# Latent attention of a four-layer kernel: queries four pairs ahead instead of eight, turn of the next rows in slot 2, second keys in slot 5

## The chip, the cores and the metric

The kernel runs on one core of one Trainium2 chip, with float32 data in and out. The metric is the device time in microseconds (us) of one execution. The engines are TensorE (PE in the rows; its weight loads are PEld), VectorE (DVE), ScalarE (ACT), GpSimd (POOL) and SyncE (SP, which issues the transfers). Each runs its own list of instructions in order and waits on semaphores.

## The reference

Four layers work on x of 4 x 256 tokens x 256 features. Each layer adds an attention-like step and a feed-forward step, each behind its own layer norm and gate. The parts around the change are the second layer's:

```python
def _L1_xattn_ref(hidden_q, kv_c, Wq, w_kc_q, w_kc_kv, W_qr, W_kr, Wo):
    ...
    q_r = jnp.einsum('bshq,hqr->bhsr', q_big, W_qr)
    k_r = jnp.einsum('bld,hdr->bhlr', kv_rope, W_kr)
    scores = jnp.einsum('bhsr,bhlr->bhsl', q_r, k_r)
    attn = jax.nn.softmax(scores, axis=-1)
    ctx_c = jnp.einsum('bhsl,bld->bhsd', attn, kv_rope)
    ctx_lat = jnp.einsum('bhsd,hkd->bshk', ctx_c, w_kc_kv)
    out = ctx_lat.reshape(b, s, H * K) @ Wo.T
    return out

def _L1_ffn_ref(x, w1, w2, w3):
    def _quantize(w):
        gamma = jnp.mean(jnp.abs(w))
        return jnp.clip(jnp.round(w / (gamma + EPS)), -1.0, 1.0)
    ...
    x1 = _bitlinear(x, w1)
    x2 = _bitlinear(x, w2)
    hidden = jax.nn.sigmoid(x1) * x2
    return _bitlinear(hidden, w3)
...
x = x + jnp.tanh(g_xattn[1]) * _L1_xattn_ref(_layernorm(x, axis=-1), ctx_512, ...)
x = x + jnp.tanh(g_ffn[1]) * _L1_ffn_ref(_layernorm(x, axis=-1), L1_ffn_w1, L1_ffn_w2, L1_ffn_w3)
```

## The kernel before

The program runs in phases: a beginning, "moe" (first layer), "latent" (the attention above), "ternary" (the feed-forward above), and "late" (the last two layers). All work of a phase is in fixed lists, one for each engine, written out in loops. The tables `latent_fills` and its like say which of the eight PSUM banks a step fills and in which order, and the semaphores `filled` and `drained` count the fills and their evacuations.

**The latent phase** has 4 batches x 8 pairs of heads = 32 items (`ITEMS1`), n = 8b + p. For item n, TensorE computes the queries of the pair (L1676, from the folded weights NW and the transposed rows XT), the scores (L1692, banks 0/1 or 2/3), the turned probabilities (L1708, eight transposes, banks 4 and 5), the values (L1720, bank 6) and the output (L1735, accumulated over the eight pairs in bank 7). VectorE takes the maximum (L1237), waits for ScalarE's four exponentials (L827), takes the reciprocal (L1244) and multiplies (L1246). ScalarE also evacuates the turned probabilities, the outputs of the values and the queries (all L710). The loop of TensorE for slot n is: turned(n), values(n-1), scores(n+2), sometimes a turn, query(n+8), output(n-2). VectorE works at n+2 in slot n: maximum(n+2), then exactly one scale(n+2).

**A turn** is the way in for the next batch: VectorE's statistics of a batch's rows (`stats`, L1013 to L1017), GpSimd's reciprocal root (`rstd`, L562 and L564), VectorE's normalised rows XN (L1025), four transposes (L1664) and ScalarE's copy to XT (L745). In the loop a turn uses bank 6, as queries do. VectorE runs the statistics two slots before the turn and XN one slot before it. Batch 1's statistics, XN and turn are done before the loop. The last turn, of slot 20, is for the ternary phase: its rows are batch 0's, with batch 0's latent output added.

**The way into the phase** on TensorE is: keys of batches 0 and 1 (four transposes, L1655), queries 0 and 1, scores 0, queries 2 and 3, scores 1, the turn of batch 1, the keys of batches 2 and 3, queries 4 to 7. Then comes the loop, whose turned(0) waits for VectorE's product 0 and for the evacuation of query 7.

**GpSimd** has one list too. In it, the `rstd` of the ternary phase's first rows comes right ahead of the ternary weights: two memsets (L595), then twelve operations that compare w1, w2 and w3 with their thresholds and subtract the results (L603, L605, L609), then three that split batch 0's transposed rows in bfloat16 parts (L617, L619, L621). The ternary phase's first matmul, `up1(0)` (L1752), stands in slot 31 of the latent loop, behind output(29) and ahead of values(31). It waits for all twelve operations and for the parts:

```python
            for b in range(NB):
                rstd(next_no("latent", b))
            pool.wait_ge(filled[6], fill("moe", 6, NB - 1, 0))
            for v in VC:
                pool.memset(v, 0.0).then_inc(pads_set, 1)
...
                if g == 0:
                    pe.wait_ge(ternary_ready, 12)
                if k == 0:
                    pe.wait_ge(parts_ready, b + 1)
```

Of the kernel before, what the change touches and what calls it, by code (L numbers as in the profile page):

```python
# [26 lines left out]
NB = 4  # L27
# [9 lines left out]
PAIRS0 = -(-CH0 // 2)  # L37
# [19 lines left out]
TURN_AT = 11  # L57
# [52 lines left out]

PAIRS1 = NH // 2
ITEMS1 = NB * PAIRS1
Q_AHEAD = PAIRS1
TURN1_AT = 4


def latent_fills():


    order = [(7, "kr", 0, 0), (4, "q", 0, 0), (5, "q", 0, 1), (0, "s", 0, 0), (4, "q", 0, 2), (5, "q", 0, 3),  # L120
             (2, "s", 0, 1), (7, "turn", 0, 0), (6, "kr", 1, 0)]
    order += [(4 + i % 2, "q", 0, i) for i in range(4, PAIRS1)]
    for n in range(ITEMS1 + 2):
        if n < ITEMS1:
            order.append((4, "t", n // PAIRS1, n % PAIRS1))
        if 1 <= n <= ITEMS1:
            order.append((6, "o", (n - 1) // PAIRS1, (n - 1) % PAIRS1))
        if n + 2 < ITEMS1:
            order.append((2 * (n % 2), "s", (n + 2) // PAIRS1, (n + 2) % PAIRS1))
        if n % PAIRS1 == TURN1_AT and n // PAIRS1 + 1 < NB:  # L130
            order.append((6, "turn", n // PAIRS1 + 1, 0))
        if n + Q_AHEAD < ITEMS1:
            order.append((6, "q", (n + Q_AHEAD) // PAIRS1, n % PAIRS1))
        if n >= 2 and (n - 2) % PAIRS1 == 0:
            order.append((7, "y", (n - 2) // PAIRS1, 0))
    return order
# [140 lines left out]
def build(nc, a, out):  # L277
    with ExitStack() as ctx:
# [404 lines left out]
        def _(act):  # L683
# [157 lines left out]
                evacuate("latent", "o", n // PAIRS1, n % PAIRS1, (OT1[:, n % 2, :], PS[:, 6, 0:S]))  # L841

            keys_out(0)
            for m in range(4):
                query_out(m)
            exponents(0)
            latent_turned(0)
            keys_out(1)
            for m in (4, 5):
                query_out(m)  # L850
            exponents(1)
            for m in range(6, PAIRS1):
                query_out(m)
            for n in range(ITEMS1 + 1):
                if n < ITEMS1:
                    turned_out(n)
                if n:
                    outputs_out(n - 1)
                if n % PAIRS1 == TURN1_AT and n // PAIRS1 + 1 < NB:
                    latent_turned(n // PAIRS1 + 1)  # L860
                if n + Q_AHEAD < ITEMS1:
                    query_out(n + Q_AHEAD)
                if n + 2 < ITEMS1:
                    exponents(n + 2)
                if n == ITEMS1 - 1:
                    hidden_tanh(0)
# [119 lines left out]
        def _(dve):  # L986
# [150 lines left out]
            for b in range(NB):  # L1137
                bank, value = fill_at("moe", "router", b)
                dve.wait_ge(filled[bank], value)
                dve.tensor_reduce(NMAX[:, :], PS[:, 7, 0:2 * E0].rearrange("p (a e) -> p a e", a=2), AX, ALU.max,  # L1140
                                  negate=True).then_inc(nmax_ready, 1)
                dve.wait_ge(drained[bank], value)
                link(dve.reciprocal(RZ[:, :], Z[:, :]))
                for i in range(2):
                    last = dve.tensor_scalar(SC[:, i, 0:E0], EX[:, i, :], RZ[:, i:i + 1], None, ALU.mult)
                link(last)
                for i in range(2):
                    last = dve.max(T8[:, i, :], SC[:, i, 0:E0])
                link(last)

                link(dve.memset(T8[:, :, K0:8], LOW))
                for i in range(2):
                    last = dve.match_replace(REP[:, i, :], T8[:, i, :], SC[:, i, :], 0.0)
                link(last)
                link(dve.tensor_tensor(CM[:, :, 0:E0], SC[:, :, 0:E0], REP[:, :, 0:E0], ALU.subtract))
                link(dve.tensor_reduce(SU[:, :], CM[:, :, 0:E0], AX, ALU.add))
                link(dve.tensor_scalar(SU[:, :], SU[:, :], 1e-20, None, ALU.add))
                link(dve.reciprocal(SU[:, :], SU[:, :]))
                for i in range(2):
                    last = dve.tensor_scalar(CM[:, i, 0:E0], CM[:, i, 0:E0], SU[:, i:i + 1], 0.5,  # L1160
                                             ALU.mult, ALU.mult)
                link(last)

                link(dve.tensor_copy(C3[:, :, 0:PART], CM[:, :, :]))
                link(dve.tensor_tensor(REP[:, :, 0:PART], CM[:, :, :], C3[:, :, 0:PART], ALU.subtract))
                link(dve.tensor_copy(C3[:, :, PART:2 * PART], REP[:, :, 0:PART]))
                dve.tensor_tensor(C3[:, :, 2 * PART:3 * PART], REP[:, :, 0:PART], C3[:, :, PART:2 * PART],
                                  ALU.subtract).then_inc(comb_ready, 1)
                for c in range(PAIRS0):
                    g, m, n = c % 2, P, 512  # L1170
                    if c == PAIRS0 - 1:
                        m, n = F0 % P, S
                    dve.wait_ge(tanh_ready, b * PAIRS0 + c + 1)
                    dve.scalar_tensor_tensor(gated[0:m, 0:n], tanh_g[0:m, g, 0:n], 1.0, PS[0:m, g, 0:n],
                                             ALU.add, ALU.mult).then_inc(drained[g], 1)
                    dve.wait_ge(drained[g], fill("moe", g, b, c // 2))
                    dve.wait_ge(filled[2 + g], fill("moe", 2 + g, b, c // 2))
                    dve.tensor_tensor(hidden[0:m, 0:n], gated[0:m, 0:n], PS[0:m, 2 + g, 0:n], ALU.mult) \
                        .then_inc(drained[2 + g], 1)
                    dve.wait_ge(drained[2 + g], fill("moe", 2 + g, b, c // 2))  # L1180
                    dve.wait_ge(filled[4 + g], fill("moe", 4 + g, b, c // 2))

                    if c >= 2:
                        dve.wait_ge(h_used, b * (PAIRS0 - 1) + c - 1)
                    dve.tensor_tensor(H[0:m, g, :, :].rearrange("p a s -> p (a s)")[:, 0:n], hidden[0:m, 0:n],  # L1185
                                      PS[0:m, 4 + g, 0:n], ALU.mult).then_inc(drained[4 + g], 1)
                    if b + 1 < NB:

                        if c == 0:
                            stats(b + 1)  # L1190
                        for r in ROUNDS_AT.get(c, ()):
                            graph_round(b + 1, r)
                        if c == 4:
                            graph_norm(b + 1)
                        if c == 7:
                            graph_mask(b + 1)
                        if c == GRAPH_AT - 1:
                            graph_add(b + 1)
                    else:
                        if c == 2:  # L1200
                            weight_sums()
                        if c == GRAPH_AT - 1:
                            thresholds()
                    if c == GRAPH_AT - 1:
                        stats((b + 1) % NB)
                    if c == GRAPH_AT:
                        normalise(after_moe(b), (b + 1) % NB,
                                  fill_at("moe", "turn", b - 1)[1])
                    if b == NB - 1 and c == TURN_AT:
                        stats(1)  # L1210
                    if b == NB - 1 and c == PAIRS0 - 1:
                        latent_next(0)
                add_residual("moe", b, TG[:, 4:5])
            v_total[0] = done[0] + done[1]

# [38 lines left out]
            for n in range(ITEMS1 + 2):  # L1254
                b, p = n // PAIRS1, n % PAIRS1
                if n + 2 < ITEMS1:
                    latent_maximum(n + 2)
                    if p == TURN1_AT - 2 and b + 1 < NB:
                        stats((b + 2) % NB)
                    if p == TURN1_AT - 1 and b + 1 < NB:  # L1260
                        latent_next(b + 1)
                    latent_scale(n + 2)
                if PAIRS1 <= n < ITEMS1 and p == 1:
                    output("latent", b - 1, TG[:, 1:2])
# [199 lines left out]
        def _(pe):  # L1464
# [232 lines left out]
            def latent_turned(n):  # L1697
# [1 line left out]
                pe.wait_ge(probs_scaled, n + 1)  # L1699
                bank = begin("latent", "t", n // PAIRS1, n % PAIRS1)  # L1700
                if n == 0:
                    at_, query = fill_at("latent", "q", 0, PAIRS1 - 1)
                    pe.wait_ge(drained[at_], query)
                for e in range(2):
                    for t in range(2):
# [72 lines left out]
            latent_query(2)  # L1778
            latent_query(3)
            latent_scores(1)  # L1780
            latent_turn(0)
            latent_keys(1)
            for m in range(4, PAIRS1):
                latent_query(m)
            for n in range(ITEMS1 + 2):
                if n < ITEMS1:
                    latent_turned(n)
# [1 line left out]
                    latent_values(n - 1)  # L1789
                if n + 2 < ITEMS1:  # L1790
                    latent_scores(n + 2)
                if n % PAIRS1 == TURN1_AT and n // PAIRS1 + 1 < NB:
                    latent_turn(n // PAIRS1 + 1)
                if n + Q_AHEAD < ITEMS1:
                    latent_query(n + Q_AHEAD)
                if n >= 2:
# [346 lines left out]
```

## Time and profile before

| what | us |
|---|---|
| median of 3 runs (lowest, highest) | 828.22 (827.05, 830.11) |
| the profiled execution, its own time | 828.94 |
| its span, first to last instruction | 826.9 |
| TensorE busy | 785.8 (95%) |
| VectorE, ScalarE, GpSimd busy | 504.7, 357.5, 155.0 |
| mean granted clock of TensorE | 0.983 of full |

The profile is of one execution. Its rows give the start in us from the span's start, the duration, the engine, the line, the operation, and in brackets how long the engine was idle before it and for whom. A row can merge several instructions (x8), and its duration then runs over all of them. TensorE's matmuls are pipelined, so the start of the next row is the better end of a row. The latent phase lies between 342 and 518 us.

### The profile page before, as it was taken

Reading aid. Unit: us, or ns where it says so; the run is one execution under the profiler, and the core shown is the slowest. Engines: PE = TensorE matmul, PEld = TensorE weight load, DVE = VectorE, ACT = ScalarE, POOL = GpSimd, SP = SyncE. Lnnn points to the kernel's source line nnn. Section 1 sums busy time; section 2 is a strip of 40 time slices with the busy share of each in tenths; the row PEclk is TensorE's granted clock in tenths of the full one; section 3 lists DMA queues with packets and bytes.
Section 4 is the critical chain, followed back from the end, with each engine's and each line's share of the span. In section 5 each row is a group of like instructions: output and inputs, shape, how many; then the busy total and the mean of one; then the engine's idle time right before and its main releaser. Section 6 shows DMA issues by size and latency. Waiting matters only on the chain.

```text
span 826.9 us, 13605 instructions
## 1 busy us (share of the span) xinstructions
PE 785.8 (95%) x5086; PEld 607.9 (74%) x5086; DVE 504.7 (61%) x1187; ACT 357.5 (43%) x1175; POOL 155.0 (19%) x160
## 2 busy tenths in 40 slices
PE   6899999999999999989999789999999999999984
PEld 3678888888888888866767556787667776777663
DVE  5656555965886564555656764333777856756763
ACT  2121112101111101366767466222888867767751
POOL 0000021000000000000002990223244332332110
PEclk9989999999999999999999899999999999999998
DMA  8945100000002000320000000000000000000000
GB/s 248 337 152 200 34 0 1 1 1 1 0 1 105 1 1 0 130 66 1 1 1 2 1 1 1 1 2 1 2 1 2 1 2 2 2 1 2 14 15 25
DMA packets 16177, 28.06 MB, mean 34 GB/s; under 512 B 3648, under 2 KB 11824, under 8 KB 15856
## 3 DMA queue, kind: packets, MB, share of 16 engines
q1 hardware_dynamic: 16112, 27.19, 10.1%
q8 instruction: 41, 0.67, 0.4%
q14 instruction: 24, 0.20, 0.1%
HBM read 26.13 MB, written 1.05 MB: 33 GB/s over the span
## 4 chain that ended last, share of the span: by engine, by line
PE 84%; DVE 7%; ACT 6%; issue 2%; POOL 1%; DMA 0%; POOLq 0%; SPq 0%; ACTq 0%; DVEq 0%
PE PS L1584 21%; PE PS L1608 10%; PE PS L1820 6%; PE PS L1844 5%; PE PS L1752 4%; PE PS L1676 3%; PE PS L1870 3%; ACT arena L827 3%; PE PS L1767 3%; PE PS L1692 2%; PE PS L1720 2%; PE PS L1708 2%; PE PS L1735 2%; PE PS L1933 2%; DVE arena L1246 2%
## 5 line engine op out<-in xcount | busy, mean ns | idle before, releaser
L710 ACT ACTIVATE arena<-PS 128x256 f32<-128x256 f32 (+3 forms) x192 | 103.2, 561 | 77.6 <-PE PS L1676 37.4
L562 POOL TENSOR_TENSOR RS<-MV,eps 128x2 f32<-128x2 f32 x32 | 6.3, 196 | 578.5 <-DVE MV L1017 517.5
L897 ACT ACTIVATE arena<-PS,W_d 128x256 f32<-128x256 f32 (+1 forms) x256 | 111.2, 453 | 6.6 <-DVE W_d L1291 6.0
L770 ACT ACTIVATE tanh_g<-PS 128x512 f32<-128x512 f32 x48 | 28.7, 599 | 180.8 <-PE PS L1584 180.8
L1584 PE MATMUL PS<-XT,W_g 128*128 128x256 f32 (+1 forms) x400 | 97.4, 386 | 0.0
L1584 PE MATMUL PS<-XT,W_u 128*128 128x256 f32 (+1 forms) x400 | 95.4, 381 | 0.0
L1608 PE MATMUL PS<-W_d,mlp_tmp 128*128 128x256 f32 (+1 forms) x400 | 94.1, 379 | 0.0
L1185 DVE TENSOR_TENSOR mlp_tmp<-mlp_tmp,PS 128x512 f32<-128x512 f32 (+1 forms) x52 | 34.7, 667 | 82.7 <-PE PS L1595 82.2
L1584 PEld LDWEIGHTS PS<-XT,W_u 128*128 128x128 f32 (+1 forms) x400 | 76.1, 190 | 11.0
L1584 PEld LDWEIGHTS PS<-XT,W_g 128*128 128x128 f32 (+1 forms) x400 | 75.2, 192 | 10.7 <-issue 0.8
L1608 PEld LDWEIGHTS PS<-W_d,mlp_tmp 128*128 128x128 f32 (+1 forms) x400 | 72.2, 190 | 8.7
L827 ACT ACTIVATE arena<-PS,arena 128x256 f32<-128x256 f32 x128 | 59.0, 478 | 13.2 <-DVE arena L1237 11.2
L1844 PE MATMUL PS<-ident,arena 128*128 128x128 f32 x448 | 61.2, 277 | 0.0
L1844 PEld LDWEIGHTS PS<-ident,arena 128*128 128x128 f32 x448 | 48.9, 141 | 10.6 <-issue 10.2
L897 ACT ACTIVATION_READ_ACCUMULATOR arena<-PS,W_d 128x1 f32 x256 | 54.3, 212 | 0.0
L1301 DVE COPY arena<-PS 128x512 f32<-128x512 f32 (+1 forms) x64 | 39.5, 617 | 14.8 <-PE PS L1844 14.8
L1291 DVE TENSOR_REDUCE W_d<-PS 128x4 f32<-128x1024 f32 x32 | 39.1, 1221 | 13.9 <-PE PS L1820 13.8
L1246 DVE TENSOR_TENSOR arena<-arena 128x1024 f32<-128x1024 f32 x32 | 44.4, 1389 | 1.1
L1237 DVE TENSOR_REDUCE arena<-PS 128x4 f32<-128x1024 f32 x32 | 39.1, 1222 | 9.0 <-PE PS L1692 6.8
L1244 DVE RECIPROCAL arena<-arena 128x4 f32<-128x4 f32 x32 | 5.7, 177 | 59.9 <-ACT arena L827 59.9
L1676 PE MATMUL PS<-XT,NW 128*128 128x256 f32 x128 | 35.6, 408 | 4.0 <-ACT XT L745 2.5
L1708 PE MATMUL PS<-ident,arena 128*128 128x128 f32 x256 | 34.4, 278 | 4.0 <-DVE arena L1246 2.8
(213 smaller groups left out, 1377.1 us busy)
## 6 DMA issues: line engine op xcount, KB each, us to landing
W_d<-in_w_d SPq DMA_DIRECT2D x1, 3072.0 KB, 10.5
arena<-in_wq SPq DMA_DIRECT2D x4, 512.0 KB, 7.2
arena<-in_wo1T SPq DMA_DIRECT2D x4, 512.0 KB, 9.0
W_g<-in_w_g SPq DMA_DIRECT2D x2, 1024.0 KB, 12.3
W_u<-in_w_u SPq DMA_DIRECT2D x2, 1024.0 KB, 14.2
arena<-in_wkq1T SPq DMA_DIRECT2D x4, 384.0 KB, 8.2
mlp_w<-in_w SPq DMA_DIRECT2D x1, 1408.0 KB, 6.0
W_g<-in_w_g SPq DMA_DIRECT2D x1, 1120.0 KB, 8.7
```

Source lines behind the costliest of these rows:

```text
L710: last = act.activation(dst, src, ACT.Copy)
L827: last = act.activation(PR[:, n % 2, k * S:(k + 1) * S], PS[:, bank + e, i * S:(i + 1) * S], ACT.Exp, bias=NM1[:, n % 2, k:k + 1], accum_o ...
L897: last = act.activation(PL[:, n % 2, k * S:k * S + w], PS[:, bank + x, i * S:i * S + w], ACT.Exp, bias=NML[:, n % 2, k:k + 1], accum_out=D ...
L1237: dve.tensor_reduce(NM1[:, n % 2, :], PS[:, bank:bank + 2, :].rearrange("p e (i s) -> p (e i) s", i=2), AX, ALU.max, negate=True).then_inc ...
L1246: dve.tensor_tensor(rows, rows, DEN1[:, n % 2, :].unsqueeze(2).to_broadcast([P, 4, S]), ALU.mult) \
L1301: dve.tensor_copy(PLT[:, n % 4, 512:512 + w], PS[:, bank, 0:w]).then_inc(drained[bank], 1)
L1584: last = mm(PS[0:m, k, e * S:(e + 1) * S], w[:, d, f0:f0 + m], XT[p][:, d, :], start=d == 0, stop=d == 1)
L1608: last = mm(PS[:, 6, i * D:(i + 1) * D], H[0:m, c % 2, e, i * P:(i + 1) * P], W_d[0:m, f, :], start=f == 0 and i == 0, stop=f == CH0 - 1, ...
L1676: last = mm(PS[:, bank, 0:S], NW[:, c, i * P:(i + 1) * P], XT[b % 2][:, c, :], start=c == 0, stop=c == 1)
L1708: last = pe.transpose(PS[:, bank + e, t * S + i * P:t * S + (i + 1) * P], PR[:, n % 2, col:col + P], ident[:, :])
L1820: last = mm(PS[:, bank + x, i * S:i * S + w], QM[r % 2][rows, e, c, i * P:(i + 1) * P], keys[rows, c, 0:w], start=i == 0 or not causal(r), ...
L1844: last = pe.transpose(PS[:, bank + x, t * S + (i - first) * P:t * S + (i - first + 1) * P], PL[:, n % 2, col:col + P], ident[:, :])
```

## The change

`Q_AHEAD` goes from 8 to 4: query(n+4) stands in slot n's place of query(n+8), and queries 4 to 7 move from the way in to slots 0 to 3. `TURN1_AT` goes from 4 to 2, and a turn stands in each of the four batches: slots 2, 10, 18 and 26. The turns are for batch 1, batch 2, batch 3 and the ternary phase's first rows. Before, the last three of them were in slots 4, 12 and 20. The keys of batches 2 and 3 move from the way in to slot 5 (bank 6). VectorE's statistics and XN move with the turns: slots 0, 8, 16, 24 and 1, 9, 17, 25. Batch 1's leave the end of the moe phase. GpSimd's list keeps its order; what it waits for moves.

```diff
-Q_AHEAD = PAIRS1
-TURN1_AT = 4
+Q_AHEAD = 4
+TURN1_AT = 2
+KEYS1_AT = 5
...
-             (2, "s", 0, 1), (7, "turn", 0, 0), (6, "kr", 1, 0)]
-    order += [(4 + i % 2, "q", 0, i) for i in range(4, PAIRS1)]
+             (2, "s", 0, 1)]
...
 (ScalarE)
-            for m in range(4):
+            for m in range(3):
                 query_out(m)
             exponents(0)
-            latent_turned(0)
-            keys_out(1)
-            for m in (4, 5):
-                query_out(m)
+            query_out(3)
             exponents(1)
-            for m in range(6, PAIRS1):
-                query_out(m)
...
 (VectorE, end of moe)
-                    if b == NB - 1 and c == TURN_AT:
-                        stats(1)
-                    if b == NB - 1 and c == PAIRS0 - 1:
-                        latent_next(0)
...
 (VectorE, latent loop)
-                    if p == TURN1_AT - 2 and b + 1 < NB:
-                        stats((b + 2) % NB)
-                    if p == TURN1_AT - 1 and b + 1 < NB:
-                        latent_next(b + 1)
+                    if p == TURN1_AT - 2:
+                        stats((b + 1) % NB)
+                    if p == TURN1_AT - 1:
+                        latent_next(b)
...
 (TensorE)
             latent_scores(1)
-            latent_turn(0)
-            latent_keys(1)
-            for m in range(4, PAIRS1):
-                latent_query(m)
...
-                if n % PAIRS1 == TURN1_AT and n // PAIRS1 + 1 < NB:
-                    latent_turn(n // PAIRS1 + 1)
+                if n % PAIRS1 == TURN1_AT and n < ITEMS1:
+                    latent_turn(n // PAIRS1)
+                if n == KEYS1_AT:
+                    latent_keys(1)
                 if n + Q_AHEAD < ITEMS1:
                     latent_query(n + Q_AHEAD)
```

In the listings below the changed kernel's lines are 5 lower on TensorE and VectorE's loop (L1703 is L1708 of before, L1671 is L1676, L1659 is L1664, L1232 is L1237, L1239 is L1244, L1241 is L1246, L1224 is L1229) and 1 lower for the statistics and XN (L1024 is L1025).

TensorE on the way into the phase, before, from scores 1 to slot 1's turned probabilities:

```order
L1692 MATMUL PS<-KR,arena 128x256 x4
L1664 MATMUL PS<-ident,XN 128x128 x4
L1655 MATMUL PS<-ident,VV 128x128 x4
L1676 MATMUL PS<-XT,NW 128x256 x8
L1708 MATMUL PS<-ident,arena 128x128 x8
L1692 MATMUL PS<-KR,arena 128x256 x4
L1676 MATMUL PS<-XT,NW 128x256 x2
L1708 MATMUL PS<-ident,arena 128x128 x8
```

The same place in the changed kernel, up to the first turn:

```order
L1687 MATMUL PS<-KR,arena 128x256 x4
L1703 MATMUL PS<-ident,arena 128x128 x8
L1687 MATMUL PS<-KR,arena 128x256 x4
L1671 MATMUL PS<-XT,NW 128x256 x2
L1703 MATMUL PS<-ident,arena 128x128 x8
L1715 MATMUL PS<-arena,VV 64x256 x4
L1687 MATMUL PS<-KR,arena 128x256 x4
L1671 MATMUL PS<-XT,NW 128x256 x2
L1703 MATMUL PS<-ident,arena 128x128 x8
L1715 MATMUL PS<-arena,VV 64x256 x4
L1687 MATMUL PS<-KR,arena 128x256 x4
L1659 MATMUL PS<-ident,XN 128x128 x4
```

Between scores 1 and turned(0), the turn, the keys and eight matmuls of four queries are gone; the first turn comes behind scores 4 in slot 2.

VectorE in slots 24 and 25 (maximum 26 to maximum 28), before:

```order
L1237 TENSOR_REDUCE arena<-PS 128x4
L1244 RECIPROCAL arena<-arena 128x4
L1246 TENSOR_TENSOR arena<-arena 128x1024
L1237 TENSOR_REDUCE arena<-PS 128x4
L1244 RECIPROCAL arena<-arena 128x4
L1246 TENSOR_TENSOR arena<-arena 128x1024
L1229 SCALAR_TENSOR_TENSOR X<-PS,TG,X 128x512
L1237 TENSOR_REDUCE arena<-PS 128x4
```

The same place in the changed kernel, from maximum 26 to product 27:

```order
L1232 TENSOR_REDUCE arena<-PS 128x4
L1012 BN_STATS BN<-X 128x6
L1013 BN_STATS BN<-X 128x6
L995 MEMSET carrier 128x1
L1015 BN_AGGR MV<-BN 128x2
L1016 BN_AGGR MV<-BN 128x2
L1239 RECIPROCAL arena<-arena 128x4
L1241 TENSOR_TENSOR arena<-arena 128x1024
L1232 TENSOR_REDUCE arena<-PS 128x4
L1024 TENSOR_SCALAR XN<-X,MV,RS 128x256 x2
L1239 RECIPROCAL arena<-arena 128x4
L1241 TENSOR_TENSOR arena<-arena 128x1024
```

The statistics of the ternary phase's first rows, which before stood behind maximum 20 (slot 18), stand behind maximum 26 (slot 24), and their XN behind maximum 27.

## Rows read from the trace of the kernel before

**Rows 1.** The page: its first line, and the chain of waits by engine.

```profile
span 826.9 us, 13605 instructions
PE 84%; DVE 7%; ACT 6%; issue 2%; POOL 1%; DMA 0%; POOLq 0%; SPq 0%; ACTq 0%; DVEq 0%
```

**Rows 2.** Timeline, TensorE, way into the phase: start, us, engine, line, operation, count, [idle].

```profile
348.72 0.66 PE L1664 MATMUL PS<-ident,XN 128*128 128x128 f32 x4
...
349.64 3.62 PE L1676 MATMUL PS<-XT,NW 128*128 128x256 f32 x16
...
354.48 1.06 PE L1708 MATMUL PS<-ident,arena 128*128 128x128 f32 x8 [1.21 <-ACT arena L710]
```

**Rows 3.** Timeline, VectorE, way into the phase: product 0.

```profile
350.22 1.22 DVE L1246 TENSOR_TENSOR arena<-arena 128x1024 f32<-128x1024 f32 x1
```

**Rows 4.** Timeline, TensorE, slots 4 (with a turn) and 5 of the loop.

```profile
375.54 0.66 PE L1664 MATMUL PS<-ident,XN 128*128 128x128 f32 x4
376.88 1.13 PE L1676 MATMUL PS<-XT,NW 128*128 128x256 f32 x4 [0.69 <-ACT XT L745]
377.85 1.03 PE L1735 MATMUL PS<-PM,arena 128*128 128x256 f32 x4
378.71 1.04 PE L1708 MATMUL PS<-ident,arena 128*128 128x128 f32 x8
...
383.58 1.04 PE L1708 MATMUL PS<-ident,arena 128*128 128x128 f32 x8
```

**Rows 5.** Timeline, TensorE, slots 25 and 26, which have no query.

```profile
485.86 1.09 PE L1708 MATMUL PS<-ident,arena 128*128 128x128 f32 x8 [0.35 <-DVE arena L1246]
...
490.44 1.09 PE L1708 MATMUL PS<-ident,arena 128*128 128x128 f32 x8 [0.35 <-DVE arena L1246]
```

**Rows 6.** Timeline, VectorE, from the ternary phase's statistics (slot 18) on.

```profile
449.55 0.15 DVE L1017 BATCH_NORM_AGGREGATE MV<-BN 128x2 f32<-128x6 f32 x1
...
453.11 7.24 DVE L1025 TENSOR_SCALAR XN<-X,MV,RS 128x256 f32<-128x256 f32 x2
...
460.47 4.06 DVE L1246 TENSOR_TENSOR arena<-arena 128x1024 f32<-128x1024 f32 x1
...
477.60 3.62 DVE L1246 TENSOR_TENSOR arena<-arena 128x1024 f32<-128x1024 f32 x1
```

**Rows 7.** Timeline, GpSimd, first, second and fifth operation of the ternary weights, last of the parts.

```profile
450.69 1.85 POOL L595 MEMSET W_d<- 128x1024 f32 x2
452.51 3.85 POOL L603 TENSOR_SCALAR mlp_tmp<-mlp_w,thr 128x1408 f32<-128x1408 f32 x1
...
463.55 4.69 POOL L603 TENSOR_SCALAR mlp_tmp<-mlp_w,thr 128x1408 f32<-128x1408 f32 x1
...
493.98 2.01 POOL L621 TENSOR_TENSOR W_d<-mlp_tmp,W_d 128x512 bf16<-128x512 f32 x1
```

**Rows 8.** Timeline, TensorE, slots 19, 20 and 26: its longer waits, and up1(0).

```profile
448.55 1.04 PE L1708 MATMUL PS<-ident,arena 128*128 128x128 f32 x8
...
460.41 1.12 PE L1664 MATMUL PS<-ident,XN 128*128 128x128 f32 x4 [3.63 <-DVE XN L1025]
462.70 2.08 PE L1676 MATMUL PS<-XT,NW 128*128 128x256 f32 x4 [1.18 <-ACT XT L745]
464.57 1.65 PE L1735 MATMUL PS<-PM,arena 128*128 128x256 f32 x4
...
495.79 1.31 PE L1735 MATMUL PS<-PM,arena 128*128 128x256 f32 x4 [2.17 <-DVE X L1229]
...
518.39 1.47 PE L1752 MATMUL PS<-W_d 128*128 128x256 bf16 x12
```

**Rows 9.** Stretches: us, busy of PE, PEld, DVE, ACT, POOL, granted clock, DMA share, GB/s.

```profile
453.00:466.00 13.00, 8.19 (x40) 5.87 (x39) 12.63 (x6) 5.18 (x15) 12.82 (x4) 0.74 0.01 3
...
493.00:500.00 7.00, 4.83 (x24) 3.33 (x22) 4.36 (x6) 4.65 (x14) 2.84 (x3) 0.76 0.00 0
...
516.00:540.00 24.00, 24.00 (x172) 19.02 (x171) 8.61 (x26) 6.28 (x14) 4.73 (x7) 1.00 0.01 1
```

More of the change, by code:

```diff
@@ L129, in latent_fills @@
             order.append((2 * (n % 2), "s", (n + 2) // PAIRS1, (n + 2) % PAIRS1))
-        if n % PAIRS1 == TURN1_AT and n // PAIRS1 + 1 < NB:
-            order.append((6, "turn", n // PAIRS1 + 1, 0))
+        if n % PAIRS1 == TURN1_AT and n < ITEMS1:
+            order.append((6, "turn", n // PAIRS1, 0))
+        if n == KEYS1_AT:
+            order.append((6, "kr", 1, 0))
         if n + Q_AHEAD < ITEMS1:
-            order.append((6, "q", (n + Q_AHEAD) // PAIRS1, n % PAIRS1))
+            order.append((6, "q", (n + Q_AHEAD) // PAIRS1, (n + Q_AHEAD) % PAIRS1))
         if n >= 2 and (n - 2) % PAIRS1 == 0:
@@ L858, in _ @@
                     outputs_out(n - 1)
-                if n % PAIRS1 == TURN1_AT and n // PAIRS1 + 1 < NB:
-                    latent_turned(n // PAIRS1 + 1)
+                if n % PAIRS1 == TURN1_AT and n < ITEMS1:
+                    latent_turned(n // PAIRS1)
+                if n == KEYS1_AT:
+                    keys_out(1)
                 if n + Q_AHEAD < ITEMS1:
@@ L1701, in latent_turned @@
                 if n == 0:
-                    at_, query = fill_at("latent", "q", 0, PAIRS1 - 1)
+                    at_, query = fill_at("latent", "q", 0, Q_AHEAD - 1)
                     pe.wait_ge(drained[at_], query)
@@ L1791, in _ @@
                     latent_scores(n + 2)
-                if n % PAIRS1 == TURN1_AT and n // PAIRS1 + 1 < NB:
-                    latent_turn(n // PAIRS1 + 1)
+                if n % PAIRS1 == TURN1_AT and n < ITEMS1:
+                    latent_turn(n // PAIRS1)
+                if n == KEYS1_AT:
+                    latent_keys(1)
                 if n + Q_AHEAD < ITEMS1:
```

## The prediction, made before the run

> **What bounds the kernel now.** I read the page first: one chain of work ended last, and 84% of it is TensorE [rows 1]. So a stretch in which TensorE is never idle ends sooner only if it has less work, and any wait of TensorE that is added ahead of such a stretch is paid in full. Then I read the timeline of the latent phase engine by engine. Three things are to be seen there. On the way in, TensorE is busy from 348.72 to about 353.3, waits 1.21 us, and starts turned(0) at 354.48 [rows 2], although VectorE's product 0 ended at 350.22 + 1.22 = 351.44 [rows 3]. In the loop a slot with a query takes 383.58 - 378.71 = 4.87 us with TensorE never idle [rows 4], and one without a query 490.44 - 485.86 = 4.58 us, in which TensorE waits for VectorE [rows 5]. So the softmax chain (maximum, exponentials, product) has a period of 4.58, and a query costs 377.85 - 376.88 = 0.97 of TensorE. Last, GpSimd gets its long list of ternary weights when VectorE's statistics of slot 18 end, at 449.55 + 0.15 = 449.70 [rows 6], and ends it, with batch 0's parts, at 493.98 + 2.01 = 495.99 [rows 7]: 46.3 us. Its consumer, up1(0), starts at 518.39 [rows 8]. That is 22.4 us of slack, and it is what the change spends.
>
> **The way in.** Between scores 1 and turned(0) the turn, the keys and four queries are gone. Turned(0) can then start when product 0 is there, about 0.1 us behind 351.44, at 351.55: product 0 doesn't get earlier, since it stands behind maximum 1, which needs scores 1, and scores 1 keeps its place. Gain: 354.48 - 351.55 = 2.9 us. VectorE's statistics and XN that leave the end of the first phase are worth nothing, because TensorE is busy there; in slots 0 and 1 the exponentials hide them.
>
> In exchange TensorE is idle from 348.72 to 351.55, 2.8 us. The trace has idle times of 2.17 and 3.63 us in this phase [rows 8]; around both, the granted clock was 0.76 and 0.74 of full, that is partly at 1.2 GHz instead of 2.4 [rows 9]. The second one cost, beyond the wait, (1.12 - 0.66) + (2.08 - 1.13) + (1.65 - 1.03) = 2.0 us [rows 4, 8]. I expect the same fall here, between 0 and 2.0 us, and take 1.2, because the first slots have waits for ScalarE that can swallow some of it.
>
> **The turns and the keys.** In the loop a turn costs what stands between its start and that of the query behind it, 376.88 - 375.54 = 1.34 us, since the query needs bank 6 back from ScalarE [rows 4]. The first turn now is in the loop: +1.34. The keys are the same four transposes, copy and bank: +1.34. The other three turns only move (slots 4, 12, 20 to 10, 18, 26).
>
> **The queries.** Four of them leave the way in (in the 2.9 us above) and stand in slots 24 to 27 at the end. Each of these slots then takes 4.87 in place of 4.58: 4 x 0.29 = +1.2 us, if TensorE were the one that decides there. Without GpSimd the change would be close to nothing: -2.9 + 1.2 + 2.7 + 1.2 = +2.2 us.
>
> **GpSimd's list.** The statistics that release it move from slot 18 to slot 24. Where is slot 24's end in the changed kernel? Before, turned(19) started at 448.55 [rows 8], and the statistics ended 1.15 us after that. Turned(25) now starts at 448.55 - 2.9 (way in) + 6 x 4.87 (six slots more) + 1.34 (two turns lay ahead before, now three) + 1.34 (keys) + 1.2 (clock) = 478.7, and the statistics end at 479.9.
>
> How long does the list take? Before, 46.3 us, in which VectorE made seven products. A product and an operation of GpSimd don't run together: XN took 7.24 us, one product 4.06 and one 3.62, where they arrived just behind the start of an operation of GpSimd [rows 6], and GpSimd's comparison took 4.69 where it had a product ahead of it and 3.85 where it had not [rows 7]. So each product costs GpSimd 0.84 us. The list alone is 46.3 - 7 x 0.84 = 40.4; with the five products that now follow the statistics and its XN (27 to 31) it is 44.6, and I take 45.0. The end is 479.9 + 45.0 = 524.9, 6.5 us behind up1(0)'s 518.39.
>
> The Trainium skill says the same of the two engines ("SBUF — State Buffer", "Who interferes with whom"): whoever issues first holds the shared port pair for its whole instruction, and the other fully blocks. The trace agrees: XN's two instructions, 0.73 us elsewhere, took 7.24. By that rule GpSimd can't be stretched beyond the waits counted above, nor shortened below its own work.
>
> Is TensorE late there anyway? From 478.7 it needs 4.87 for slot 25; 4.87 + 1.34 + 6.1 for slot 26, which now has the turn that waits for XN as slot 20 did (3.63 idle, 1.18 - 0.69 more for XT, 2.0 of clock) [rows 4, 8]; 4.87 for slot 27; 3 x 4.58 for 28 to 30; and some 3.0 up to up1(0): 517.5. Then it waits 7.4 us. The products that meet an operation of GpSimd (about 2.4 us each: 3.62 - 1.22) use up this wait first. Idle time before up1(0) brings the lower clock again; I take the 2.0 us of above once more, bounds 0 and 2.8. From there on TensorE was busy for 24.00 of 24.00 us [rows 9], so nothing takes the delay back.
>
> **Sum.** +6.5 (up1(0) later) + 2.0 (clock behind the wait) = +8.5 us. Way in, turns and clock at the start are inside the 6.5. Against the profiled execution's own 828.94 this is 837.4; that execution was 0.7 above the median of 828.22, so 836.7.
>
> **Rivals.**
>
> 1. *GpSimd's list is at its shortest.* If the products cost it nothing because they fall into its gaps, it takes 40.4, and up1(0) is at 520.4. With no fall of the clock on the way in, 519.2. That is +0.8 to +2.0, plus clock 1 to 2: 830 to 832. For it: the products adapt to GpSimd's period. Against: 4.69 in place of 3.85 where a product came between. Chance 0.16.
>
> 2. *Faster: TensorE sets the end.* Then the gain on the way in counts and the fuller slots 24 to 27 cost little: 517.5 - 518.4 = -0.9, and without the fall of the clock on the way in -2.1: 826 to 827. The wait of 2.17 us for batch 2's output in slot 26 [rows 8], which is merged with the turn's wait, is in that sum. The point from which it decides: the list must take less than 517.5 - 479.9 = 37.6 us, which is below its own 40.4, or the statistics must end 3 us earlier than I think. Chance 0.05.
>
> 3. *Slower still: VectorE's chain ends behind GpSimd.* Each product that just misses its turn costs 2.4 to 3.5 us. With three or four such misses in slots 26 to 31, turned(31) is late and up1(0) is at 527 to 529, +10 to +12 with the clock: 838.5 to 841. Before there was one such product beside XN and the one behind it. Chance 0.12.
>
> 4. *The change doesn't do what it says*, for instance since the statistics still come early. The order shows them in slot 24; chance 0.01.
>
> **Numbers.** The forecast has 0.66: up1(0) waits for GpSimd's list, 833 to 840 with its bounds (clock 0 to 2.0 on the way in and 0 to 2.8 behind the wait, list 43 to 46.3). The range, 831 to 841, takes in most of rivals 1 and 3 and leaves out rival 2. About 0.5% (4.1 us) is what a measurement of this kernel can tell from no change: slower by more than that is above 832.4, which is the forecast and rival 3 and little of rival 1, 0.80; within is most of rival 1 and part of the others, 0.15; faster 0.05.
>
> **What would show it.** In the profile of the changed kernel: turned(0) at about 351.5, with about 2.8 us idle before it and a granted clock below 1 behind it; slots of 4.87 up to slot 27; statistics ending at about 480; XN of slot 25 at some 7 us; GpSimd's last part ending at about 525; TensorE idle for several us ahead of up1(0), and waiting for GpSimd; the ternary phase as long as before. The prediction is wrong if up1(0) starts without a wait for GpSimd, if the list takes under 40 us, or if the delay at up1(0) isn't found again in the span.

## The result, and the profile after

| | before | changed |
|---|---|---|
| median of 8 runs each | 829.22 (827.05 to 831.93) | 834.69 (829.55 to 835.28) |
| ratio, 95% interval | | 1.006 (1.0037 to 1.0083) |
| the profiled execution | 828.94, span 826.9 | 835.25, span 833.2 |

The change makes the kernel slower, by some 5 us; the interval lies above 1. The forecast was 836.7 in a range from 831 to 841. These are the rows of the changed kernel that answer to the ones ahead. First TensorE's timeline on the way in, at the keys of slot 5, at turned(25), in slots 26 to 29, and at up1(0) (columns as in [rows 2]; lines are 5 lower than before's):

```profile
342.17 0.60 PE L1650 MATMUL PS<-ident,VV 128*128 128x128 f32 x4
...
351.22 1.09 PE L1703 MATMUL PS<-ident,arena 128*128 128x128 f32 x8 [2.67 <-DVE arena L1241]
352.25 1.65 PE L1687 MATMUL PS<-KR,arena 64*128 64x256 f32 x8
353.82 2.07 PE L1671 MATMUL PS<-XT,NW 128*128 128x256 f32 x4
355.69 1.27 PE L1703 MATMUL PS<-ident,arena 128*128 128x128 f32 x8
...
380.02 0.66 PE L1650 MATMUL PS<-ident,VV 128*128 128x128 f32 x4
381.37 1.13 PE L1671 MATMUL PS<-XT,NW 128*128 128x256 f32 x4 [0.69 <-ACT KR L712]
...
478.53 1.04 PE L1703 MATMUL PS<-ident,arena 128*128 128x128 f32 x8
...
489.81 1.12 PE L1659 MATMUL PS<-ident,XN 128*128 128x128 f32 x4 [3.29 <-DVE XN L1024]
492.10 2.07 PE L1671 MATMUL PS<-XT,NW 128*128 128x256 f32 x4 [1.17 <-ACT XT L747]
494.75 2.04 PE L1730 MATMUL PS<-PM,arena 128*128 128x256 f32 x4 [0.57 <-DVE X L1224]
496.58 1.92 PE L1703 MATMUL PS<-ident,arena 128*128 128x128 f32 x8
498.43 1.60 PE L1715 MATMUL PS<-arena,VV 128*64 128x256 f32 x8
...
502.85 1.04 PE L1703 MATMUL PS<-ident,arena 128*128 128x128 f32 x8
...
509.23 1.52 PE L1703 MATMUL PS<-ident,arena 128*128 128x128 f32 x8 [2.21 <-DVE arena L1241]
510.68 1.98 PE L1715 MATMUL PS<-arena,VV 128*64 128x256 f32 x8
...
523.53 1.47 PE L1747 MATMUL PS<-W_d 128*128 128x256 bf16 x12 [1.61 <-issue]
```

Turned(0) starts at 351.22, 2.67 us after the last work of TensorE, and the score and query matmuls behind it are slow. The keys of slot 5 cost 381.37 - 380.02 = 1.35 us. Turned(25) starts at 478.53. The last row is up1(0), 5.1 us later than before's 518.39 [rows 8].

GpSimd's timeline, from the start of the list to the end of the parts (answers to [rows 7]), and VectorE's, from the statistics on (answers to [rows 6]):

```profile
480.11 1.84 POOL L597 MEMSET W_d<- 128x1024 f32 x2
481.93 3.84 POOL L605 TENSOR_SCALAR mlp_tmp<-mlp_w,thr 128x1408 f32<-128x1408 f32 x1
...
492.95 4.69 POOL L605 TENSOR_SCALAR mlp_tmp<-mlp_w,thr 128x1408 f32<-128x1408 f32 x1
...
522.28 1.15 POOL L623 TENSOR_TENSOR W_d<-mlp_tmp,W_d 128x512 bf16<-128x512 f32 x1
```

```profile
478.97 0.15 DVE L1016 BATCH_NORM_AGGREGATE MV<-BN 128x2 f32<-128x6 f32 x1
...
482.83 6.93 DVE L1024 TENSOR_SCALAR XN<-X,MV,RS 128x256 f32<-128x256 f32 x2
...
489.87 4.06 DVE L1241 TENSOR_TENSOR arena<-arena 128x1024 f32<-128x1024 f32 x1
...
498.06 3.82 DVE L1241 TENSOR_TENSOR arena<-arena 128x1024 f32<-128x1024 f32 x1
...
505.23 3.94 DVE L1241 TENSOR_TENSOR arena<-arena 128x1024 f32<-128x1024 f32 x1
```

The statistics end at 478.97 + 0.15 = 479.12, the list at 522.28 + 1.15 = 523.43, and up1(0) starts 0.1 us behind it: TensorE waits for GpSimd. XN took 6.93 us (7.24 before, in slot 19), and three products met an operation of GpSimd, where before it was two (4.06 and 3.62, [rows 6]).

Granted clock (columns as in [rows 9]) of the way in and of slot 26 with what follows:

```profile
348.00:360.00 12.00, 8.99 (x53) 6.02 (x50) 7.96 (x14) 7.49 (x25) 0.88 (x2) 0.86 0.63 212
...
488.00:500.00 12.00, 8.44 (x30) 5.61 (x30) 9.90 (x7) 4.42 (x12) 11.82 (x4) 0.57 0.00 0
```

The span grew by 6.3 us, and up1(0) came only 5.1 later. The rest comes later, nearly all of it at the very end of the program. From the chain of waits (start, us, what), the same eight matmuls of the last output projection, before and then changed:

```profile
804.55 2.01 PE PS L1933 x8
```

```profile
809.58 3.30 PE PS L1926 x8
```

Both have a wait of 0.83 us ahead. The granted clock of the 4 us there, before and then changed:

```profile
804.50:808.50 4.00, 3.22 (x16) 2.58 (x17) 2.90 (x12) 0.64 (x2) 0.00 (x0) 1.00 0.02 4
```

```profile
809.50:813.50 4.00, 3.92 (x12) 2.86 (x12) 1.73 (x8) 0.00 (x0) 0.00 (x0) 0.58 0.00 0
```

In one execution TensorE was at 2.4 GHz there, in the other mostly at 1.2. That is 1.29 us. The instructions there are the same in both kernels, and the time from up1(0) to the end was 308.0 to 310.1 us over all ten profiles of this text without following the length of the phase (310.1 in the first experiment below, 309.7 in the changed kernel). So I don't count these 1.29 us to the change; that is an argument from the profiles, no run tests it.

### The profile page after: what moved, and what is told of

Its sections match the earlier page's. It is cut to its first block, busy times and chain, and to the rows that moved or that the text cites. A ratio compares the mean times of both kernels' runs of the same rounds, so it can differ in the third digit from the quotient of the medians.

```text
span 833.2 us, 13605 instructions
## 1 busy us (share of the span) xinstructions
PE 790.2 (95%) x5086; PEld 611.2 (73%) x5086; DVE 508.0 (61%) x1187; ACT 356.1 (43%) x1175; POOL 152.9 (18%) x160
## 4 chain that ended last, share of the span: by engine, by line
PE 87%; DVE 6%; ACT 4%; issue 2%; POOL 1%; DMA 0%; POOLq 0%; SPq 0%; ACTq 0%; DVEq 0%
PE PS L1579 21%; PE PS L1603 10%; PE PS L1813 6%; PE PS L1837 5%; PE PS L1747 4%; PE PS L1671 4%; PE PS L1687 4%; PE PS L1715 3%; PE PS L1863 3%; PE PS L1703 3%; PE PS L1730 3%; PE PS L1762 3%; PE PS L1926 2%; PE PS L1590 1%; PE PS L1532 1%
## 5 line engine op out<-in xcount | busy, mean ns | idle before, releaser
L1241 DVE TENSOR_TENSOR arena<-arena 128x1024 f32<-128x1024 f32 x32 | 47.3, 1480 | 1.1
L1232 DVE TENSOR_REDUCE arena<-PS 128x4 f32<-128x1024 f32 x32 | 39.2, 1224 | 8.5 <-PE PS L1687 7.7
L1239 DVE RECIPROCAL arena<-arena 128x4 f32<-128x4 f32 x32 | 5.7, 177 | 59.2 <-ACT arena L829 59.2
L1671 PE MATMUL PS<-XT,NW 128*128 128x256 f32 x128 | 37.5, 420 | 4.3 <-ACT XT L747 3.2
L1703 PE MATMUL PS<-ident,arena 128*128 128x128 f32 x256 | 34.9, 281 | 5.6 <-DVE arena L1241 5.6
```

The lines of the kernel that those rows point to most:

```text
L1232: dve.tensor_reduce(NM1[:, n % 2, :], PS[:, bank:bank + 2, :].rearrange("p e (i s) -> p (e i) s", i=2), AX, ALU.max, negate=True).then_inc ...
L1241: dve.tensor_tensor(rows, rows, DEN1[:, n % 2, :].unsqueeze(2).to_broadcast([P, 4, S]), ALU.mult) \
L1671: last = mm(PS[:, bank, 0:S], NW[:, c, i * P:(i + 1) * P], XT[b % 2][:, c, :], start=c == 0, stop=c == 1)
L1703: last = pe.transpose(PS[:, bank + e, t * S + i * P:t * S + (i + 1) * P], PR[:, n % 2, col:col + P], ident[:, :])
```

## The experiments

The time up to the phase's first matmul varied by some 3.8 us between profiles (339.35 to 343.16), and the time from up1(0) to the end by 2.1 (308.0 to 310.1). So beside the times I read from each trace the **phase**: from the first keys (first row above; L1655 before) to up1(0). All from one profile of each kernel; the ratios are against the kernel before on the same chips. The phase too has parts that vary between executions: the clock on the way in is worth 1.4 us of it (see the part on the prediction), so small differences between phases are no more than hints.

| kernel | phase, us | median (runs) | ratio, 95% interval |
|---|---|---|---|
| before | 518.39 - 342.40 = 176.0 | | |
| changed | 523.53 - 342.17 = 181.4 | 834.69 (8) | 1.006 (1.0037 to 1.0083) |
| e1_last_turn_20 | 514.90 - 339.40 = 175.5 | 828.48 (12) | 1.0004 (0.999 to 1.0018) |
| e2_queries_only | 512.92 - 339.35 = 173.6 | 827.75 (12) | 0.9982 (0.9965 to 1.0) |
| e3_list_behind_xn | 525.31 - 341.43 = 183.9 | 838.89 (4) | 1.0123 (1.0085 to 1.0161) |
| e4_short_list | 520.09 - 343.16 = 176.9 | 829.14 (10) | 1.0013 (0.9998 to 1.0027) |
| e5_before_list_behind_xn | 514.96 - 341.83 = 173.1 | 825.06 (6) | 0.9957 (0.9941 to 0.9973) |
| e6_q4_wait | 512.83 - 342.10 = 170.7 | 823.42 (6) | 0.9934 (0.9915 to 0.9953) |
| e6_q5_wait | 514.17 - 343.10 = 171.1 | 824.31 (6) | 0.9947 (0.9931 to 0.9962) |
| e6_q6_wait | 513.33 - 341.54 = 171.8 | 825.84 (8) | 0.997 (0.9954 to 0.9985) |

### The last turn alone put back

```diff
+TURNS1 = {2: 0, 10: 1, 18: 2, 20: 3}
...
-                if n % PAIRS1 == TURN1_AT and n < ITEMS1:
-                    latent_turn(n // PAIRS1)
+                if n in TURNS1:
+                    latent_turn(TURNS1[n])
```

The same edit stands in ScalarE's loop and the table of fills; VectorE's `stats` and `latent_next` go by `n + 2 in TURNS1` and `n + 1 in TURNS1`.

> The changed kernel with one thing put back: the last turn (the ternary phase's first rows) is in slot 20 again, with its statistics in slot 18 and its XN in slot 19; the other turns stay in slots 2, 10 and 18, the second keys in slot 5, queries four ahead. Theory (GpSimd's list, released by those statistics, sets up1(0)): the list is released near 449 us and ends near 496, so up1(0) no longer waits for it; up1(0) starts near 520.5 instead of 523.5, the time is 2 to 3 us below the changed kernel's, ratio to before about 1.003. Rival (the turns, keys and queries that stand in the loop cost the time by themselves, and the list only happens to end late): up1(0) stays at 523 or later and the ratio stays at 1.006.

Measured: phase 175.5, ratio 1.0004. GpSimd's list and TensorE's up1(0), from their timelines:

```profile
445.85 1.84 POOL L598 MEMSET W_d<- 128x1024 f32 x2
...
490.25 1.16 POOL L624 TENSOR_TENSOR W_d<-mlp_tmp,W_d 128x512 bf16<-128x512 f32 x1
```

```profile
514.90 1.47 PE L1748 MATMUL PS<-W_d 128*128 128x256 bf16 x12
```

The list ends 23.5 us ahead of up1(0), which doesn't wait. The last turn, moved by six slots, makes a difference of 181.4 - 175.5 = 5.9 us. Of these, 1.4 are the clock on the way in, which stayed high in this execution, long before the turn that was moved; the 4.5 that are left agree with the ratios (1.006 against 1.0004, some 4.6 us), and that is nearly all of the loss. The 2 to 3 us that I had expected were too few: I had counted the low clock on the way in as lost here too, and also full slots 24 to 27, but these took 499.44 - 478.76 = 20.7 us from turned(24) to turned(28), against 502.36 - 481.28 = 21.1 before. The wait of 2.17 us for batch 2's output [rows 8] is down to 0.60 in this kernel.

### The queries alone

```diff
-Q_AHEAD = PAIRS1
+Q_AHEAD = 4
...
-            for m in range(4, PAIRS1):
+            for m in range(4, Q_AHEAD):
                 latent_query(m)
```

With the same bounds in the table of fills and in ScalarE's list; the turn and the keys stay on the way in.

> The kernel before with the queries alone changed: four pairs ahead instead of eight. The turn of batch 1 and the second keys stay on the way in, the other turns in slots 4, 12 and 20. Theory: turned(0) starts 2.9 us earlier, near 351.5, behind 1.9 us of idle time; slots 24 to 27 hold a query again (+1.2 us at most); GpSimd's list starts 2 to 3 us earlier and is never waited for; up1(0) starts at 516.7 to 518.5, ratio 0.998 to 1.001. Rival (queries four ahead are what costs, since they fill slots 24 to 27 or lower the clock on the way in): up1(0) at 521 or later, ratio 1.003 or more.

Measured: phase 173.6, ratio 0.9982. TensorE, end of the way in:

```profile
346.16 0.60 PE L1655 MATMUL PS<-ident,VV 128*128 128x128 f32 x4
348.44 1.09 PE L1708 MATMUL PS<-ident,arena 128*128 128x128 f32 x8 [1.69 <-DVE arena L1246]
```

Turned(0) comes 348.44 - 339.35 = 9.1 us after the first keys; before it was 354.48 - 342.40 = 12.1. Of this gain of 3.0 us, 2.4 are left at up1(0), so in the loop the queries cost 0.6 us net. It is made of two parts. Slots 24 and 25 took 486.53 - 475.53 = 11.0 us, against 490.44 - 481.28 = 9.2 before; that is 1.8 us, more than I had put for all four queries. Most of it comes back behind slot 25, where the wait for batch 2's output is 0.61 us instead of 2.17 [rows 8] and the clock doesn't fall behind it:

```profile
491.31 1.10 PE L1735 MATMUL PS<-PM,arena 128*128 128x256 f32 x4 [0.61 <-DVE X L1229]
492.25 1.04 PE L1708 MATMUL PS<-ident,arena 128*128 128x128 f32 x8
```

The interval reaches 1.0, so by the time alone this is not told from no change. The profiled execution was the shortest of the twelve (823.41 us); its phase began 3.0 us earlier than before's, which the phase's own length doesn't hold. The first experiment has one turn and the keys more in the loop than the second, and its turns of batches 2 and 3 stand six slots later. From turned(0) to turned(19), that is before GpSimd's list, it takes 445.07 - 348.46 = 96.6 us against 443.03 - 348.44 = 94.6, and the phases differ by 175.5 - 173.6 = 1.9. So the turn and the keys cost 1.9 to 2.0 us in the loop, against the 2.7 in the sum.

### GpSimd's list later still

```diff
             pool.wait_ge(filled[6], fill("moe", 6, NB - 1, 0))
+            pool.wait_ge(xn_ready, next_no("latent", NB - 1) + 1)
             for v in VC:
                 pool.memset(v, 0.0).then_inc(pads_set, 1)
```

> The changed kernel, in which GpSimd starts its list of ternary weights only when VectorE has written the XN of slot 25. XN and GpSimd's comparison then don't meet: XN takes 0.7 us instead of 6.9, and TensorE's waits in slot 26 (3.3 for XN, part of 1.2 for XT) and the low clock behind them go. Theory (the list sets up1(0)): TensorE gains some 5 us and nothing comes of it; the list starts and ends 3.5 us later, near 527, up1(0) starts there and waits 8 us or more, and the time is 3 to 5.5 us above the changed kernel's (ratio to before 1.010 to 1.013). Rival (TensorE's waits for VectorE in slots 26 to 31 set the end): the time falls by 4 to 5 us, ratio 1.000 to 1.001.

Measured: phase 183.9, ratio 1.0123. VectorE's XN, GpSimd's list and TensorE's up1(0):

```profile
482.23 0.73 DVE L1025 TENSOR_SCALAR XN<-X,MV,RS 128x256 f32<-128x256 f32 x2
```

```profile
483.07 1.84 POOL L598 MEMSET W_d<- 128x1024 f32 x2 [3.52 <-DVE XN L1025]
...
524.06 1.15 POOL L624 TENSOR_TENSOR W_d<-mlp_tmp,W_d 128x512 bf16<-128x512 f32 x1
```

```profile
525.31 2.72 PE L1748 MATMUL PS<-W_d 128*128 128x256 bf16 x12 [9.08 <-issue]
527.96 1.44 PE L1716 MATMUL PS<-arena,VV 128*64 128x256 f32 x8
```

XN is at its own 0.73 us, TensorE no longer waits for it, and the kernel is slower: TensorE's time went into a wait of 9.08 us. That is the test that tells the theories apart, and the rival, 1.000, is out. The medians are 4.2 us apart, as expected; the phases only 2.5, from one profile each. The clock behind the wait was low: up1(0) and the values took 2.65 and 1.37 us from start to start, where they take 1.40 and 1.01 in the changed kernel, 1.6 us together.

### A shorter list

```diff
+                some = 64 if k == 1 else n
-                pool.tensor_scalar(less[0:parts, 0:n], wf, thr[0:parts, 1, c:c + 1], None, ALU.is_lt) \
+                pool.tensor_scalar(less[0:parts, 0:some], wf[:, 0:some], thr[0:parts, 1, c:c + 1], None, ALU.is_lt) \
```

The second comparison likewise.

> The changed kernel with a shorter list on GpSimd: the two comparisons of the second half of w1 and w2 work on 64 of their 1408 columns, so the weights of the ternary phase are not the reference's. It is for the price of the list. Theory: the list gets 7 us shorter, ends near 516, and TensorE's own chain decides; up1(0) starts at 518 to 522, and the time is 1.5 to 5 us below the changed kernel's (ratio 1.000 to 1.004). Rival (the list isn't waited for): no change against the changed kernel, ratio 1.006.

Measured: phase 176.9, 4.4 us below the changed kernel's; ratio 1.0013. GpSimd's last operation is over at 518.05, 2.0 us before up1(0) at 520.09, which now has no wait:

```profile
516.03 2.02 POOL L624 TENSOR_TENSOR W_d<-mlp_tmp,W_d 128x512 bf16<-128x512 f32 x1
```

```profile
520.09 1.47 PE L1748 MATMUL PS<-W_d 128*128 128x256 bf16 x12
```

So TensorE's own chain is nearly the kernel before's length (176.0), and what is above it in the changed kernel is the list, by its wait of 1.61 us and by the products that the full list delays. Behind XN's own, the products that met an operation of GpSimd took 2.43 us here (the one at 505.44), and 3.82 and 3.94 in the changed kernel.

### The same wait where the list has slack

The edit of the third experiment, in the kernel before.

> The kernel before with one wait added: GpSimd starts its list of ternary weights only when VectorE has written the XN of slot 19. It is the wait of the run e3_list_behind_xn, put where the list has slack. Theory (the list matters only once its slack is spent; here it has 22 us): the list starts and ends 3.5 us later, near 499, and still isn't waited for; XN takes 0.7 instead of 7.2 us, TensorE's 3.6 us for it and the low clock behind go; the phase from the first keys to up1(0), 176.0 before, takes 170 to 172, ratio 0.993 to 0.996. Rival (TensorE's wait for XN is made up elsewhere in the phase): 175 to 176, ratio 1.000.

Measured: phase 173.1, ratio 0.9957, faster. VectorE's XN and products (timeline), with those that pass freely left out:

```profile
452.47 0.73 DVE L1026 TENSOR_SCALAR XN<-X,MV,RS 128x256 f32<-128x256 f32 x2
...
461.51 2.48 DVE L1247 TENSOR_TENSOR arena<-arena 128x1024 f32<-128x1024 f32 x1
467.33 4.04 DVE L1247 TENSOR_TENSOR arena<-arena 128x1024 f32<-128x1024 f32 x1
...
479.33 3.90 DVE L1247 TENSOR_TENSOR arena<-arena 128x1024 f32<-128x1024 f32 x1
```

One wait on GpSimd makes the kernel slower where the list is due (1.0123 against 1.006) and faster where it isn't. Slot 20 took 459.72 - 453.01 = 6.7 us from turned(20) to turned(21), against 466.06 - 453.67 = 12.4 before. The phase gained only 2.9 us, half of that: three products now meet an operation of GpSimd for long (2.48, 4.04, 3.90), where before it was two (4.06, 3.62). The phase is 1 us above the theory's range and 2 below the rival's; I had taken the later list for harmless to the products.

### Both gains together, and how many queries ahead

```diff
-Q_AHEAD = PAIRS1
+Q_AHEAD = 4
...
+            pool.wait_ge(xn_ready, next_no("latent", NB - 1) + 1)
```

With the other bounds as in the second experiment; the other two kernels have 5 and 6.

> Queries four ahead alone (as in e2_queries_only, phase 173.6) together with GpSimd's wait for XN. Theory: the two gains add, since one is on the way in and the other at slot 20: phase 167.5 to 169.5, ratio 0.990 to 0.993. Rival: the products that meet the later list lose the gain again, 171 or more, ratio 0.995 or more.

> As e6_q4_wait with queries five ahead: query 4 stays on the way in, in 0.9 of the 1.7 us in which TensorE waits for product 0. Theory: turned(0) starts as early, and one query less stands in the loop (0.97 us of TensorE where it decides): phase 0 to 0.7 us below e6_q4_wait's. Rival: nothing, since slot 27's query fits under the softmax chain anyway.

> As e6_q4_wait with queries six ahead: queries 4 and 5 on the way in. TensorE's wait for product 0 is then filled (1.8 us), but turned(0) also waits for ScalarE's copy of query 5, which stands behind four exponentials, the XT copy and the keys. Theory: turned(0) starts up to 0.5 us later than with four, the phase is within 0.7 us of e6_q4_wait's. Rival: the exponentials of pair 1, behind two copies more, come 0.8 us later and delay slots 1 and 2: phase 0.5 to 1 us longer.

Measured: phases 170.7, 171.1 and 171.8; ratios 0.9934, 0.9947, 0.997. The phase gains add, 176.0 - 2.4 - 2.9 = 170.7, though the phase fell less than I had expected, as in the fifth experiment. By the ratios the sum is not told from the wait alone (0.9915 to 0.9953 and 0.9941 to 0.9973 overlap). More queries on the way in don't help. Six cost 1.1 us of the phase against four, more than the 0.7 I had allowed and near the rival's 0.5 to 1. With six, turned(0) comes 9.71 us after the first keys instead of 9.09 and waits for ScalarE's copy. With five it comes at 9.09, and the phase isn't shorter, so the query left over was not what decided. The intervals of four and five overlap; four with the wait has the lowest median here, and its interval is below both the kernel before's 1 and the changed one's.

## Why the prediction was right, and where its sum was off

**GpSimd's list sets up1(0): right.** Its release at 479.12 (forecast 479.9), its length 523.43 - 479.12 = 44.3 us (forecast 45.0), up1(0) at 523.53 (forecast 524.9). The way there held too: turned(0) at 351.22, of which 0.2 us is an earlier start of the phase, the keys at 1.35 us, turned(25) at 478.53 (forecast 478.7). The first and third experiment show the cause: with the last turn alone put back the loss is gone, and a later list costs more although TensorE loses its waits for XN.

**The clock on the way in: right in this profile.** In the changed kernel's profile the score matmuls took 1.65 us (1.13 in the first experiment) and the query 2.07 (1.13 in [rows 4]); from turned(0) to turned(1) it was 355.69 - 351.22 = 4.5 us, against 351.51 - 348.46 = 3.1 us in the first experiment, where after the same wait the clock did not fall (last section). At turned(18) it is still 1.4 us (443.05 - 351.22 = 91.8 against 438.85 - 348.46 = 90.4), so nothing swallowed it. The price is 1.4 us (forecast 1.2), and it comes and goes: that it was paid in the profiled execution was luck for the forecast of 479.9.

**Slots 24 to 27, and the loop: too dear.** The queries were put at 1.2 us and cost 0.6 net, turn and keys at 2.7 and cost 1.9 to 2.0 (first and second experiment). The term for the queries had no part for the wait of 2.17 us for batch 2's output and the low clock behind it, of which 0.61 us and no low clock were left in the second experiment. The first slots have room of their own, since TensorE waits for ScalarE there (0.53 us at 355.16 in the first experiment, 0.92 at 355.53 in the second); that this is why the turn and the keys cost less isn't shown by a run.

**TensorE ready at 517.5: wrong, and with it the term of 2.0 us for the clock.** TensorE was ready at 523.53 - 1.61 = 521.9, 4.4 us later than forecast. By the forecast's own steps turned(26) was due at 483.6 and came at 483.40. Turned(28) was due at 500.8 and came at 502.85, and it had no wait ahead: the first 2.1 us are mostly the low clock in slots 26 and 27. I had put 2.0 us for it, as in slot 20, where it was over with the output; here output, turned and values took 1.83, 1.85 and 1.52 us from start to start too, so that it cost 3.8. The rest are two products that met the list (3.82 and 3.94 us, 2.6 and 2.7 above their own 1.22), part of which fell in slack, the wait of 2.21 us ahead of turned(29), and a low clock behind it (1.98 us for the values in slot 29, the row at 510.68). I had named these misses, priced at 2.4 each, but left them out of the 517.5. So the wait ahead of up1(0) was 1.61 us instead of 7.4, and up1(0) took 1.47 us, as before: no low clock. That is the step that failed: +2.0 was added for a wait that had no room to be long. Where it was long, 9.08 us in the third experiment, the clock did fall, and it cost 1.6 us. "TensorE: Matmul & The Clock Gate", "What's actually happening", in the Trainium skill says that the throttled state is the default and activity lifts it; the rows agree in direction: full clock behind 1.61 us of idle time, a low one behind 9.08 (granted clock 0.61 from 524 to 530 us in the third experiment).

The fourth experiment agrees that the products made TensorE late: with the list 6.5 us shorter (37.8 us from the end of the statistics at 480.26 to 518.05) and only 2.43 us for a product behind XN's, the phase was 176.9 us instead of 181.4. That is 0.9 above before's, where the prediction has two prices for the change without GpSimd, +2.2 us under its queries and -0.9 in its second rival; the first leaves out that the wait of 2.17 us goes.

**The size.** The forecast was +8.5 us, without that term +6.5. Measured were +6.3 us by the spans, of which 1.3 is the clock at the program's end, and +5.5 us by the medians. That 836.7 is only 2.0 above the measured 834.69 is in part luck: the median of the kernel before, 828.22 in 3 runs, came out at 829.22 in 8.

**The rivals.** The list at its shortest, and TensorE as the one that decides, are out: the list took 44.3 us, not 40.4, and TensorE waited for it. The third rival, products that miss their turn, was half true: two of them, which is why TensorE was almost as late as GpSimd. Whether one more would have made TensorE decide was not run: 2.6 us is more than the 1.61 of wait that was left, but part of such a miss can fall in slack.

## What to carry to other kernels

Before a step is moved later, look for what it releases on an engine that is hardly busy: GpSimd was at 19%, and its list of 44 us is still the longest serial piece between its release and its consumer. Take the slack as start of the consumer minus end of the list, here 22.4 us [rows 7, 8], and compare it with how far the release moves, here 29.4. The 7.0 us between them, less the 2.0 by which the list got shorter (46.3 to 44.3), are the 5.1 at up1(0), within rounding. A wait that moves a low-priority list behind a short critical operation of the engine it blocks is worth trying wherever that slack exists, and made the kernel slower where it didn't.

## What the hardware showed that I had not expected

- The same idle time in the same place lowers TensorE's clock in one execution and not in another. After 2.67 us of idle time on the way in, the granted clock of the 12 us around it was 0.86 in the changed kernel and 0.86 in the third and fourth experiment, but 1.00 in the first, and the first query there took 1.13 us instead of 2.07. After 1.69 us (second experiment) it was 1.00. Within the third experiment turned(29) and the values behind it took 1.82 and 1.98 us after a wait of 2.66 us (501.21; granted clock of the 8 us around it 0.79), but 1.10 and 1.08 after one of 3.05 us (513.07; 1.00). What decides between the two isn't shown here. The rows of the first experiment, clock first, then TensorE's timeline:

```profile
345.00:357.00 12.00, 8.80 (x64) 6.31 (x60) 9.17 (x16) 8.41 (x30) 0.89 (x2) 1.00 0.63 221
```

```profile
348.46 1.09 PE L1704 MATMUL PS<-ident,arena 128*128 128x128 f32 x8 [2.67 <-DVE arena L1242]
349.48 1.13 PE L1688 MATMUL PS<-KR,arena 64*128 64x256 f32 x8
350.55 1.13 PE L1672 MATMUL PS<-XT,NW 128*128 128x256 f32 x4
351.51 1.04 PE L1704 MATMUL PS<-ident,arena 128*128 128x128 f32 x8
```

- At the end of the program eight matmuls took 2.01 us in one profile and 3.30 in another, with the same waits around. Differences of 1.3 us between the spans of single profiles of this kernel say nothing about a change. The length of the phase that was edited says more, but it too holds the 1.4 us of clock on the way in.
